# Three P buffers instead of four, more block sums on TensorE, and row maxima reduced into PSUM

## The reference

```python
h = layernorm(x)
q, k, v = heads(h @ Wq + bq), heads(h @ Wk + bk), heads(h @ Wv + bv)   # 16 heads of 32
att = q @ k.T / sqrt(32)
att = where(causal & (key % 4 != 3), att, -inf)                        # every 4th key is never seen
y = softmax(att) @ v
x = x + layernorm(y @ Wp + bp)
i = argmax(log_softmax(logits) - log(-log(u)))                         # one of 8 matrices
x = x + layernorm(layernorm(x) @ W[i] + b[i])
```

## Time and profile before

| | |
|---|---|
| median of 3 runs | 2431.74 us (2428.77 to 2431.99) |
| the profiled execution | 2432.43 us, its span 2430.6 us |
| TensorE busy | 2284.5 us, 94% |
| ScalarE, VectorE, GpSimd busy | 72%, 71%, 64% |
| TensorE's mean granted clock | 0.979 of full speed |
| DMA | 57 GB/s on average |

### The profile page before, as it was taken

One profiled execution on the slowest core, in us unless ns is written; L12 is line 12 of the kernel. 1 busy time (PEld: TensorE's weight loads), 2 busy tenths in 40 slices (PEclk: granted clock), 3 DMA queues, 4 the chain that ended last, 5 costly groups with the idle time before them and its releaser, 6 DMA issues.

```text
span 2430.6 us, 43417 instructions
## 1 busy us (share of the span) xinstructions
PE 2284.5 (94%) x14996; PEld 959.5 (39%) x14996; DVE 1725.1 (71%) x4774; ACT 1748.0 (72%) x3206; POOL 1558.4 (64%) x1440
## 2 busy tenths in 40 slices
PE   4899999999999998998999998999799999999897
PEld 2444433433444443433344443343244444333332
DVE  7777787675568777778267768778827677677774
ACT  7568677678767777677866867767677686776683
POOL 3247567788647567588943758668865565776644
PEclk9899999999999999999999999999999999999998
DMA  7213121121233212112141312102113221301001
GB/s 197 72 42 84 33 60 52 28 69 46 56 83 72 59 48 62 30 43 51 37 100 50 85 43 62 57 23 56 40 35 98 75 60 41 85 23 32 17 14 44
DMA packets 224358, 137.49 MB, mean 57 GB/s; under 512 B 146730, under 2 KB 196618, under 8 KB 224138
## 3 DMA queue, kind: packets, MB, share of 16 engines
q1 hardware_dynamic: 222310, 134.65, 21.8%
q10 hardware_dynamic: 1828, 0.07, 0.0%
HBM read 39.69 MB, written 16.78 MB: 23 GB/s over the span
## 4 chain that ended last, share of the span: by engine, by line
PE 68%; DVE 13%; ACT 8%; issue 6%; POOL 4%; DMA 1%; SPq 0%; POOLq 0%; ACTq 0%; DVEq 0%
PE acc L1310 12%; PE acc L1274 11%; PE acc L1294 10%; PE acc L1245 9%; PE acc L1246 8%; PE acc L1247 8%; PE acc L1325 7%; ACT P L962 5%; DVE MHL L1055 3%; DVE MP L1044 3%; DVE acc L1040 3%; POOL P L824 2%; PE acc L1298 2%; DVE STA L1021 1%; PE acc L1250 1%
## 5 line engine op out<-in xcount | busy, mean ns | idle before, releaser
L962 ACT ACTIVATE P<-acc,EX 128x512 f32<-128x512 f32 (+2 forms) x1920 | 1078.1, 640 | 297.7 <-PE acc L1298 138.4
L824 POOL TENSOR_TENSOR P<-P 128x512 f32<-128x512 f32 x732 | 908.6, 1276 | 102.0 <-PE acc L1310 72.4
L1044 DVE TENSOR_REDUCE MP<-acc 128x1 f32<-128x512 f32 (+1 forms) x1088 | 719.5, 679 | 212.2 <-PE acc L1274 208.8
L1040 DVE CUSTOM_DVE_ANT_0 acc<-acc,CB 128x96 f32<-128x96 f32 (+7 forms) x1024 | 449.9, 456 | 253.0 <-PE acc L1274 249.4
L1274 PE MATMUL acc<-KST,QST 96*128 96x512 f16 (+10 forms) x2112 | 592.7, 336 | 38.8 <-DVE MP L1040 21.5
L1294 PE MATMUL acc<-QST,KST 98*128 98x512 f16 (+2 forms) x1920 | 587.1, 357 | 32.4 <-DVE MP L1040 15.4
L1310 PE MATMUL acc<-P,V 128*32 128x512 f32 (+2 forms) x3840 | 435.5, 548 | 1.3 <-ACT P L962 1.1
L1274 PEld LDWEIGHTS acc<-KST,QST 96*128 96x128 f16 x2112 | 194.7, 98 | 352.1 <-issue 60.3
L1294 PEld LDWEIGHTS acc<-QST,KST 98*128 98x128 f16 x1920 | 183.5, 98 | 292.3 <-ACT P L962 55.8
L815 POOL TENSOR_TENSOR QKL<-SC,QKH 128x384 f16<-128x384 f32 (+1 forms) x128 | 136.3, 1065 | 211.8 <-ACT QKH L937 211.5
L803 POOL TENSOR_TENSOR RR<-RR,NHALF 128x1 f32<-128x1 f32 x256 | 144.0, 566 | 183.7 <-DVE NM L1026 183.3
(11 more groups left out here) (152 smaller groups left out, 3010.2 us busy)
## 6 DMA issues: line engine op xcount, KB each, us to landing
QST<-QKH SPq DMA_DIRECT2D x128, 128.0 KB, 3.2
XR<-in_L_attn_x_dram SPq DMA_DIRECT2D x60, 256.0 KB, 2.8
out_dram<-XR SPq DMA_DIRECT2D x60, 256.0 KB, 2.1
KST<-QKH SPq DMA_DIRECT2D x128, 96.0 KB, 2.6
XB<-in_L_attn_x_dram SPq DMA_DIRECT2D x48, 252.0 KB
QST<-QKL SPq DMA_DIRECT2D x64, 128.0 KB, 3.3
KST<-QKL SPq DMA_DIRECT2D x64, 96.0 KB, 2.7
XB<-in_L_attn_x_dram SPq DMA_DIRECT2D x20, 256.0 KB, 3.4
```

The costliest lines, as they stand in the source:

```text
L824: e.tensor_tensor(P[:, acc, a, :], P[:, acc, a, :], P[:, buf, a, :], ALU.add).then_inc(g_s, 1)
L962: e.activation(P[:, p_buf[u, g, sb_], a, t0:512], bank(*step)[:, t0:512], ACT.Exp, scale=EX[:, 1:2]).then_inc(a_e, 1)
L1040: e.tensor_tensor_reduce(out=ps, in0=ps, in1=MASKM[:, 512 - n:512], scale=1.0, scalar=-3.0e38, op0=ALU.add, op1=ALU.max, accum_out=maxima( ...
L1044: e.tensor_reduce(maxima(u, g)[:, r, a, ci:ci + 1], bank(*s)[:, 0:n], AX.X, ALU.max).then_inc(v_m, 1)
```

## The change

- `P` has three buffers. One holds the group's accumulator and the other two alternate.
- TensorE sums every block with `sb % 3 == 1` as well as the three blocks on the diagonal. Before, it was the diagonal and, for j of 2 and 3, the one or two blocks before it. The adds that are left are the blocks 2 for j = 1, the blocks 2, 3, 5 for j = 2, and 2, 3, 5, 6, 8 for j = 3; before they were 1 and 2, 1 to 4, and 1 to 6.
- The gathered maxima are no longer in `MX` but in columns 256 to 271 of a PSUM bank, and the transposes of "shift" go to columns 0 to 255 of the same bank. This bank is of a new kind, psH, of which two may be held; it is taken by "peaks" and given back when ScalarE has copied the rows. Before, "shift" took a psM bank.
- `V` has room for a fifth stretch and goes round over five; `YX` has four buffers, one for each `r`. The constants and the bias rows that stood in `YX` during the start now stand in `V`.
- The planner's durations: "peaks" 720 in place of 900 ns, "norm" on ScalarE 1000 in place of 820. "invert" is planned after the "out" before it.

```diff
 def on_pe(j, sb):
-    return sb >= 3 * j - max(j - 1, 0)
+    return sb >= 3 * j or sb % 3 == 1
...
-    ring = [0, 1, 2, 3]
+    last, acc = 2, 0
     for u in range(NB * NJ):
         for g in range(4):
+            new = [i for i in range(3) if i not in (acc, last)][0]
+            ring = [last, acc]
+            acc = first[u, g] = new
             for sb in range(3 * (u % NJ) + 3):
-                now = buf[u, g, sb] = ring.pop(0)
-                if sb:
-                    ring.append(now)
-                else:
-                    first[u, g] = now
...
+                last = acc if sb == 0 else ring[(sb - 1) % 2]
+                buf[u, g, sb] = last
...
-    MOST = {"psX": 2, "psW": 2, "psM": 3, "psS": 4, "psO": 2, "psU": 2}
+    MOST = {"psX": 2, "psW": 2, "psM": 3, "psS": 4, "psO": 2, "psU": 2, "psH": 2}
...
-            add("dve", s - 0.2, 900, ("peaks", u, g), [("dve", "peak", u, g, r, a, ci) for r, a, ci, _ in jobs],
-                [("MHL", ("pe", "shift", u, g))])
-            add("pe", s - 0.2, 300, ("shift", u, g), [("dve", "peaks", u, g)], [("psM", ("act", "shift", u, g))])
+            add("dve", s - 0.2, 720, ("peaks", u, g), [("dve", "peak", u, g, r, a, ci) for r, a, ci, _ in jobs],
+                [("MHL", ("pe", "shift", u, g)), ("psH", ("act", "shift", u, g))])
+            add("pe", s - 0.2, 300, ("shift", u, g), [("dve", "peaks", u, g)])
...
-        V = sb("V", [128, 3 * NJ, 512], F32)
+        V = sb("V", [128, 3 * (NJ + 1), 512], F32)
...
-        P = sb("P", [128, 4, 4, 512], F32)
+        P = sb("P", [128, 3, 4, 512], F32)
...
-        YX = sb("YX", [128, 3, 512], F32)
+        YX = sb("YX", [128, 4, 512], F32)
...
-                        if u >= NJ:
-                            ac.wait_ge(p_pv, PE["pv", u // NJ * NJ - 1, 3, 3 * (u % NJ) + 2])
+                        if u > 1:
+                            ac.wait_ge(p_pv, PE["pv", u - 2, 3, 3 * ((u - 2) % NJ) + 2])
...
-                        elif n > 2:
-                            ac.wait_ge(g_r, GP["add_y", *divmod(n - 3, 4)])
+                        if u:
+                            ac.wait_ge(g_r, GP["add_y", u - 1, i])
...
-                    e.tensor_reduce(MX[:, i, :, :].rearrange("p r a -> p (r a)"),
+                    mx = bank(*s)[:, 256:272].rearrange("p (r a) -> p r a", a=4)
+                    if order.emptier[s]:
+                        dv.wait_ge(*emptied(*order.emptier[s]))
+                    e.tensor_reduce(bank(*s)[:, 256:272],
                                     maxima(u, g).rearrange("p r a c -> p (r a) c"), AX.X, ALU.max).then_inc(v_m, 1)
...
-                    e.tensor_scalar(MHL[:, i, :, 0, :], MX[:, i, :, :], -1.0 / SM, None, ALU.mult, ALU.bypass).then_inc(v_m, 1)
+                    e.tensor_scalar(MHL[:, i, :, 0, :], mx, -1.0 / SM, None, ALU.mult, ALU.bypass).then_inc(v_m, 1)
...
-                    e.scalar_tensor_tensor(out=MHL[:, i, :, 1, :], in0=MX[:, i, :, :], scalar=-1.0 / SM,
+                    e.scalar_tensor_tensor(out=MHL[:, i, :, 1, :], in0=mx, scalar=-1.0 / SM,
                                            in1=MHL[:, i, :, 0, :], op0=ALU.mult, op1=ALU.subtract).then_inc(v_m, 1)
```

More of the change, by code:

```diff
@@ L36, in p_blocks @@
     buf, first, before, held = {}, {}, {}, {}
-    ring = [0, 1, 2, 3]
+    last, acc = 2, 0
     for u in range(NB * NJ):
         for g in range(4):
+            new = [i for i in range(3) if i not in (acc, last)][0]
+            ring = [last, acc]
+            acc = first[u, g] = new
             for sb in range(3 * (u % NJ) + 3):
-                now = buf[u, g, sb] = ring.pop(0)
-                if sb:
-                    ring.append(now)
-                else:
-                    first[u, g] = now
[L46 to L49, removed]
+                last = acc if sb == 0 else ring[(sb - 1) % 2]
+                buf[u, g, sb] = last
+                if last in held:
+                    before[u, g, sb] = held[last]
+                held[last] = u, g, sb
     return buf, first, before
@@ L163, in moments @@
         self.add("gp", rank, 600, ("rstd", k, u, r), [("dve", "stats", k, u, r), ("dve", "consts")])
-        self.add(self.normer(k, u), rank, 750 if self.normer(k, u) == "dve" else 820, ("norm", k, u, r), [("gp", "rstd", k, u, r)])
+        self.add(self.normer(k, u), rank, 750 if self.normer(k, u) == "dve" else 1000, ("norm", k, u, r), [("gp", "rstd", k, u, r)])
     def normer(self, k, u):
@@ L217, in front @@
         for a in range(3):
+            old = u - 2
             self.project(("v", u, a), self.place(s, -self.V + 6 * a), 512, 590, turned + [("dve", "wlow", 2)]
-                         + [("dve", "fold", 2)] * (u > 0) + ([("pe", "pv", u // NJ * NJ - 1, 3, 3 * j + 2)] if u >= NJ else []))
+                         + [("dve", "fold", 2)] * (u > 0) + ([("pe", "pv", old, 3, 3 * (old % NJ) + 2)] if u > 1 else []))
     @staticmethod
@@ L275, in attend @@
                         + ([(who, "add", u, g, added(j)[i - 1], a)] if i else [("pe", "pv", u, g, 0)]))
-            add("dve", s + 0.95, 1600, ("invert", u, g), [("pe", "sum", u, g, last)])
+            add("dve", s + 0.95, 1600, ("invert", u, g), [("pe", "sum", u, g, last)]
+                + [("dve", "out", *divmod(s - 1, 4))] * (s > 0))
             add("dve", s + 0.95, 610, ("out", u, g), [("dve", "invert", u, g), ("pe", "pv", u, g, last)],
@@ L302, in finish @@
             self.project(("p", u, r), at - 0.1, 512, 590, [("gp", "olow", u, g) for g in range(4)]
-                         + ([("sp", "store", *divmod(n - 6, 4))] if n == 4 * self.NU - 1 else
-                            [("gp", "add_y", *divmod(n - 3, 4))] if n > 2 else []))
+                         + ([("gp", "add_y", u - 1, r)] if u else []))
             self.moments(1, u, r, at, [("act", "evac", ("p", u, r))])
@@ L513, in sandwich_block @@
         RC = sb("RC", [128, 2], F32)
-        IDF = YX[:, 1, 256:384]
-        ON8 = YX[0:8, 1, 384:512]
+        IDF = V[:, 14, 256:384]
+        ON8 = V[0:8, 14, 384:512]
         IDH = sb("IDH", [128, 128], F16)
@@ L601, in sandwich_block @@
         DV = counted(order.dve, lambda s: {
-            "choose": ("p", 4 if s[-1] else 2), "consts": ("c", 8), "ident": ("c", 1), "wmax": ("p", 1), "bmax": ("p", 3),
+            "choose": ("p", 4 if s[-1] else 2), "consts": ("c", 7), "ident": ("c", 1), "wmax": ("p", 1), "bmax": ("p", 3),
             "allmax": ("p", 2), "scales": ("p", (16, 12, 6)[s[-1]] if s[0] == "scales" else 0), "wlow": ("w", 4 if s[0] == "wlow" and s[1] < 2 else 1),
@@ L832, in _ @@
                     gp.wait_ge(*resid_in(u, r))
-                    e.tensor_tensor(yx(u, r), yx(u, r), resid(u, r), ALU.add).then_inc(g_r, 1)
+                    e.tensor_tensor(YX[:, r, :], YX[:, r, :], resid(u, r), ALU.add).then_inc(g_r, 1)
                 elif kind == "add_y":
@@ L837, in _ @@
                     o = resid(u, r)
-                    e.tensor_tensor(o, o, yx(u, r), ALU.add).then_inc(g_r, 1)
+                    e.tensor_tensor(o, o, YX[:, r, :], ALU.add).then_inc(g_r, 1)
         @block.scalar
@@ L943, in _ @@
                         ac.wait_ge(d_m[(n - 1) % 4], 32 * ((n - 1) // 4 + 1))
-                    e.activation(MROW[:, :], bank(*s)[0:8, 0:256].bitcast(F16), ACT.Copy).then_inc(a_m, 1)
+                    e.activation(MROW[:, :], bank("peaks", u, g)[0:8, 0:256].bitcast(F16), ACT.Copy).then_inc(a_m, 1)
                 elif kind == "exp":
@@ L1185, in _ @@
                     dv.wait_ge(d_bp, 16)
-                    e.tensor_tensor(BP, BP, bank("fold"), ALU.add).then_inc(v_f, 1)
+                    e.tensor_tensor(V[:, 11, :], V[:, 11, :], bank("fold"), ALU.add).then_inc(v_f, 1)
                 elif kind == "fold":
@@ L1278, in _ @@
                     u, g = s[1:]
-                    half = bank(*s)[0:8, 0:256].bitcast(F16)
+                    half = bank("peaks", u, g)[0:8, 0:256].bitcast(F16)
                     pe.wait_ge(v_m, DV["peaks", u, g])
```

29 lines of the change are left out of this document (10 added, 19 removed).

## The result

The changed kernel takes 2376.1 us in the median of four runs (2373.86 to 2378.12), against 2431.9 us of the kernel before; the ratio is 0.977, 95% interval 0.9753 to 0.9787. It is 2.3% faster. Runs of the kernel before lie at one of two levels, about 2432 us at a mean clock of 0.979 or about 2447 us at 0.976, and those beside this result were all at the lower one. I had forecast 2425 us, and the range of 2398 to 2458 us does not hold the result.

A forecast was written before the change was run, and what follows sets the result against it. TensorE, busy 94% of the span, was taken as the bound. From the profiled 2432.4 us, 41.3 and 2.8 added and 51 saved gave 2425.5, so a median of 2425 us was predicted, range 2398 to 2458 us.

The forecast's parts named there:

- The sums: On TensorE: 48 more full-width sums of 0.86 us each, 41.3 us added.
- the switches: On TensorE: 28 more changes between full matmuls and column tiles, about 0.1 us each, 2.8 us added.
- The sign that I gave for them: Sign of the cost: 2688 instructions of L1317 in place of 2304, TensorE busy about 40 us more.
- The maxima in PSUM: VectorE's float16 steps read PSUM and stop waiting for GpSimd; 106 us off VectorE, 51 us off the end.
- the eight holes: TensorE's eight idle times behind a long L1055, 2.90 to 8.89 us each, 47.2 us in sum.
- the dearer PSUM reads: Rival: three VectorE instructions per step slower from PSUM, 4.4 us on the path, 2429 us; chance 0.05.
- 51 us saved: TensorE idle time removed: 47.2 us behind eight long L1055 plus some four holes of about 1 us.
- The three buffers: Exponentials on ScalarE with two P buffers in rotation: fits on average, taken as zero.
- The rival of a ring that stalls: Rival: late buffers delay exponentials and stall TensorE, 34 us over 48 groups, 2459 us; chance 0.26.
- the sign that the ring holds: ScalarE's waits before an exponential for GpSimd's adds and for L1302 and L1317 near 30 us.
- V, YX, the planner's numbers, psH: V and YX only give the planner freedom, zero; psH may make VectorE wait for a bank, also zero.
- More is won: Rival: the chain's 73 us for L1055 and 12 us of GpSimd's adds go, 2391 or 2403 us; chance 0.21.

The follow-up runs named there:

- e_psum: Kernel before with only the gathered maxima moved to PSUM and their bank psH, old sums, four P buffers: 2346.3 us, ratio 0.9614.
- e_psum_sums: Kernel before with maxima in PSUM, the 48 more sums and invert planned after out, four P buffers: 2391.4 us, ratio 0.9785.
- e_pause8: Changed kernel with twelve added VectorE reductions, about 8 us, inside the step peaks of eight groups: 2440.9 us, ratio 1.0002.
- e_psum_plan: Kernel before with maxima in PSUM, planner's 1000 ns for norm and invert planned after out: 2348.6 us, ratio 0.9612.
- e_sbuf: Changed kernel, all its lists kept, with only the gathered maxima back in SBUF: 2426.4 us, ratio 0.9946.
- e_plan: Kernel before, maxima in SBUF, with only the planner's new numbers (peaks 720, norm 1000, invert after out): 2470.5 us, ratio 1.0100.

## Why the prediction was wrong

**The sums.** 41.3 us and 2.8 us for the switches. Right with four buffers: 42 to 45 us between e_psum and e_psum_sums. In TensorE's busy time it is 44.7 us between e_psum and the change, at the same clock of 0.994. Beside three buffers a part comes back, and they cost 23 to 33 us: the ring loses 7 us with the old sums and not with the new ones. The sign that I gave for them, some 40 us more busy time, did not come: 14.7 us, as the clock gave the rest back.

**The maxima in PSUM.** The mechanism was right: the wait for GpSimd, the instruction, the eight holes. L1047 and L1049 take 174 ns, so the dearer PSUM reads did not come. The size was not: the term "51 us saved" is the step that failed. In e_psum, this part in the old kernel, it measured 86.6 us by the profiled spans (88 by the medians, 94 by the ratio). With the lists of the change, where the waits in SBUF are already shorter, the place of the maxima alone is worth 43 to 50 us. Two things were left out of the term.

- *The clock behind the holes.* 30.0 us of busy time for the same matmuls, between the kernel before and e_psum. I had the mean of 0.979 in the table and took it as a property of the chip. e_pause8 shows it as an effect of the waits: eight pauses of some 8 us give 46.7 us more idle time and 18.4 us more busy time for the same matmuls.
- *More idle time than the holes.* In e_psum TensorE's idle time fell by 56.6 us, near the 51. In the change it fell by 71.5. The other 14.9 us came with neither part by itself: the idle time is 89.5 us in e_psum, 93.0 with the new sums and four buffers, 85.1 with the old sums and three, and 74.6 with both. Which waits gave them stays open.

Together: 86.6 us won as in e_psum and 14.9 us less idle time, against 44.7 us more busy time, are the 56.8 us between the two profiled spans.

**The three buffers.** Taken as zero. The ratios cannot tell them from zero (0.9614 and 0.9636; 0.9785 and 0.977); the medians give 7 us of loss with the old sums and 15 us of gain with the new ones. That these nearly fit a zero is in part luck, since the two were never weighed. The rival of a ring that stalls did not come: ScalarE waited 4.7 us for adds and 26.4 us for L1302 and L1317, 31.1 us in all, near the 30 given as the sign that the ring holds. **V, YX, the planner's numbers, psH.** The planner's numbers have no measurable part of their own where the maxima are in PSUM (e_psum_plan). V and YX were only tried together with the ring, and psH in every kernel with the maxima in PSUM and in e_sbuf, so neither was weighed by itself.

**The rivals.** "More is won" was the one to expect, with 2391 to 2403 us, and even it was too high, since it also knew nothing of the clock. It rested on the chain's 3% for L1055, 73 us. The chain counts the wait itself; the matmuls at half clock behind it would stand in it as ordinary work of TensorE, which I did not look up.

The version to keep is neither kernel but e_psum: maxima in PSUM, with the old sums and buffers, 0.9614 of the kernel before. The change as a whole gives back 0.016 of that, 30 us by the medians: its 48 sums cost more than the three buffers return.

## What to carry to other kernels

Look at the longest duration of a cheap instruction and not at its mean: 174 ns at best and 9592 at worst is a wait that the view of waits does not show, since it lies inside the instruction. A small VectorE step on the critical path beside a busy GpSimd should read PSUM: as a scaling from SBUF to SBUF, or with two inputs in SBUF, it waits for GpSimd. And when TensorE is the bound, price a long hole at its own length plus 40 to 50% for the half clock behind it (18.4 us on 46.7 in e_pause8, 30.0 on 56.6 between the kernel before and e_psum); the same work in short pieces cost 26 us where the long ones cost 65.

## What the runs showed of the hardware

- A small VectorE instruction can wait out a whole gapless stretch of GpSimd instructions, and not only the one that runs when it starts: 9.59 us over the last two of four adds, L810 and five more adds. It did so as tensor_scalar from SBUF to SBUF (longest 9.59 us here, 12.0 us in e_plan) and as scalar_tensor_tensor with two SBUF inputs (9.58 us). It did not as tensor_reduce from SBUF to SBUF (longest 204 ns of 64), nor with its first input in PSUM (longest 176 ns).
- The stretch need not end in a gap. The L1055 that starts at 1704.34 us and takes 6.34 ends at 1710.68, when GpSimd has gone on from its adds to L803, a 128x1 instruction, at 1710.61.
- 16 columns read from PSUM and written to SBUF took 174 ns, the same as from SBUF without a wait.
- TensorE between full matmuls and column tiles: where a float16 matmul of 512 columns stands directly in front of tiles, they start 0.31 to 0.32 us after it (in the middle eight tenths of 86 places of the trace of before), and two such matmuls in a row start 0.21 to 0.22 us apart. That is 0.10 us for the change. The way back worked out from the earlier trace rows is 0.11 us. At about 0.1 us a change, an estimate, the 550 changes of the kernel before make 55 us.
